# Attention's P·V as f32 products on four column strips, with the turned probabilities leaving PSUM once

## What is computed

```python
# layer 1 (layer 3 is the same with a causal mask instead of bias and src_mask)
scores = jnp.einsum('bhqd,bhkd->bhqk', q / math.sqrt(HEAD_DIM), k)
scores = scores + attention_bias
scores = jnp.where(src_mask, -jnp.inf, scores.astype(jnp.float32))
probs = jax.nn.softmax(scores, axis=-1).astype(v.dtype)
ctx = jnp.einsum('bhqk,bhkd->bhqd', probs, v)
x = x + (ctx @ Wo + bo)
h = _ln(x) * g2 + beta2
ff = _gelu2(h @ W1 + b1) @ W2 + b2
```

## Time and profile before

| | us |
|---|---|
| three runs, median | 2738.48 |
| lowest and highest | 2730.14, 2739.05 |
| the profiled execution: span | 2737.0 |
| PE busy | 2599.0 (95%) |
| PE weight loads busy | 2214.0 (81%) |
| ACT busy | 2338.8 (85%) |
| DVE busy | 2221.9 (81%) |
| POOL busy | 1674.0 (61%) |

### The profile page before, as it was taken

One profiled execution on the slowest core, in us unless ns is written; L12 is line 12 of the kernel. 1 busy time (PEld: TensorE's weight loads), 2 busy tenths in 40 slices (PEclk: granted clock), 3 DMA queues, 4 the chain that ended last, 5 costly groups with the idle time before them and its releaser, 6 DMA issues.

```text
span 2737.0 us, 62626 instructions
## 1 busy us (share of the span) xinstructions
PE 2599.0 (95%) x20072; PEld 2214.0 (81%) x20072; DVE 2221.9 (81%) x7925; ACT 2338.8 (85%) x5285; POOL 1674.0 (61%) x1742
## 2 busy tenths in 40 slices
PE   8888999999999999999999999999999999999987
PEld 7766888888888888888888888888888888888776
DVE  5668888888888888888888888888888888888753
ACT  1567899999999999998999989999998998999865
POOL 2666666766667675666666566666666666765431
PEclk8988999999999999999999999999999999999999
DMA  6433343333333333333333333343333333333211
GB/s 230 130 96 102 91 118 108 116 102 113 96 103 115 109 114 103 110 98 101 114 112 112 103 108 101 98 119 108 113 97 114 101 100 116 109 105 102 63 31 29
DMA packets 176549, 287.96 MB, mean 105 GB/s; under 512 B 45856, under 2 KB 99104, under 8 KB 175840
## 3 DMA queue, kind: packets, MB, share of 16 engines
q1 hardware_dynamic: 176224, 283.97, 35.2%
HBM read 174.64 MB, written 8.45 MB: 67 GB/s over the span
## 4 chain that ended last, share of the span: by engine, by line
PE 71%; ACT 13%; issue 4%; SPq 4%; DVE 3%; POOL 2%; DMA 2%; ACTq 0%; DVEq 0%; POOLq 0%
PE bank L1171 15%; PE bank L1178 14%; PE bank L1199 10%; PE bank L1156 9%; PE bank L1148 8%; PE bank L1191 5%; ACT PB L990 3%; PE bank L1163 3%; SPq L411 2%; ACT PH L996 2%; PE bank L1306 2%; ACT BB L1011 2%; PE bank L1217 2%; PE bank L1218 2%; ACT AA L1011 2%
## 5 line engine op out<-in xcount | busy, mean ns | idle before, releaser
L990 ACT ACTIVATE PB<-PB,mx 128x256 f32<-128x256 f32 (+1 forms) x2048 | 834.6, 475 | 6.0 <-DVE mx L786 5.2
L794 DVE TENSOR_TENSOR PO<-bank,PH 128x384 f16<-128x384 f32 (+1 forms) x1024 | 589.4, 616 | 247.5 <-ACT PH L996 244.4
L497 POOL TENSOR_TENSOR BT<-BT,MN 128x1024 f32<-128x1024 f32 x256 | 545.9, 2137 | 174.2 <-DMA BT<-in_bias 173.4
L996 ACT ACTIVATE PH<-bank 128x384 f16<-128x384 f32 (+1 forms) x1024 | 499.0, 538 | 127.7 <-PE bank L1199 127.2
L1191 PE MATMUL bank<-Ks,Qs 96*128 96x512 f32 (+1 forms) x1024 | 519.1, 510 | 19.5 <-DMA Ks<-KU 11.9
L1199 PE MATMUL bank<-ident,PB 128*128 128x128 f32 x3584 | 484.8, 275 | 8.5 <-ACT PB L990 4.5
L1199 PEld LDWEIGHTS bank<-ident,PB 128*128 128x128 f32 x3584 | 421.2, 142 | 46.8 <-ACT PB L990 12.3
L786 DVE CUSTOM_DVE_ANT_0 PB<-bank,BT 128x256 f32<-128x256 f32 x1024 | 386.7, 416 | 37.6 <-PE bank L1191 36.2
L786 DVE CUSTOM_DVE_ANT_0 PB<-bank,caus 128x128 f32<-128x128 f32 (+1 forms) x1024 | 321.0, 351 | 22.9 <-PE bank L1191 22.5
L1217 PEld LDWEIGHTS bank<-VP,PH 128*128 128x128 f16 x3584 | 204.0, 96 | 119.2 <-issue 93.5
L1171 PE MATMUL bank<-TN,Wf 128*128 128x256 f32 x1024 | 253.9, 391 | 16.6 <-ACT BB L1011 11.4
(11 more groups left out here) (225 smaller groups left out, 5208.8 us busy)
## 6 DMA issues: line engine op xcount, KB each, us to landing
BT<-in_bias SPq DMA_DIRECT2D x256, 512.0 KB, 3.9
Qs<-QH SPq DMA_DIRECT2D x512, 64.0 KB, 2.4
Ks<-KH SPq DMA_DIRECT2D x1024, 32.0 KB, 2.0
Qs<-QU SPq DMA_DIRECT2D x256, 64.0 KB, 2.5
Ks<-KU SPq DMA_DIRECT2D x512, 32.0 KB, 2.0
XT<-in_xT SPq DMA_DIRECT2D x32, 256.0 KB, 2.9
X<-in_x SPq DMA_DIRECT2D x32, 256.0 KB, 2.9
AB<-ada_rows SPq DMA_DIRECT2D x32, 256.0 KB, 3.6
```

Source lines behind the costliest of these rows:

```text
L497: G.op.tensor_tensor(v2(BT[k % 4]), v2(BT[k % 4]), MN[:, :].unsqueeze(1).broadcast_to([128, 2, 512]), ALU.add).then_inc(g_bt, 1)
L794: V.op.tensor_tensor(PO[i][:, 0:w], bP[h][:, 0:w], PH[i][:, 0:w], ALU.subtract).then_inc(v_low, 1)
L990: S.op.activation(o, o, ACT.Exp, scale=-1.0, bias=mx[u.layer][:, c:c + 1]).then_inc(a_exp, 1)
L996: S.op.activation(PH[i][:, 0:w], bP[h][:, 0:w], ACT.Copy).then_inc(a_high, 1)
```

## The change

What it does:

- **One copy out of PSUM.** `high` and `low` are gone. The turned probabilities of head 0 are copied by ACT (`ev0`), those of head 1 by DVE (`ev1`), each once, in f32, into a ring of six tiles `PT` (`flipped`).
- **P·V turned round.** Once for a pair, `pv` issues for each half k of the keys four f32 products: the stationary side is a head's 128x32 slice of `VW` (16 channels of V and 16 columns of ones), the moving side its turned probabilities, 256 queries wide (128 in the second half of layer 3, where the causal mask leaves nothing else). The four (two units x two heads) go to four column strips of the array, `tile_position=(0, 32*s)`, and to 32 partitions each of one half of the bank `bV`.
- **A turn back.** The result has channels on partitions, so ACT copies it out (`cx`, into `ET`) and PE turns it (`ct`, two f32 transposes of 128x128 per pair) before `pvn`, which is now a reciprocal and one product.
- **V is not split.** `v_hi`, `v_sub`, `v_mid`, `v_lo` are gone; `v_out` writes f32 into `VW`.
- **Room.** `PT` needs SBUF, so `FY` becomes `XT`, `MB` becomes `TN`, `MC` becomes `AA[3]` and `TC` becomes `BB[3]` (`AA[3]` in the last batch), with five new waits: `ld_x` also waits for `v_n2`, `t2_out` for `p_w3`, `t4_out` for `p_w1`, `c3_out` for `p_w4`, and `v_out` for `p_pv` of the batch before.
- **Ticks.** All numbers of `P` and `OWN` are new, and a small table `SPLIT` gives layer 3 its own ticks for five pieces.

```diff
-    "score0": -2, "score1": 0, "bias0": 1, "bias1": 3, "exp0": 3, "exp1": 6, "flip0": 7, "flip1": 7,
-    "high0": 8, "high1": 8, "low0": 10, "low1": 10, "pv0": 12, "pv1": 12, "pvn": 15,
+    "score0": -2, "score1": 1, "bias0": -1, "bias1": 2, "exp0": 2, "exp1": 5, "flip0": 7, "flip1": 7, "ev0": 8,
+    "ev1": 8, "pv": 12, "cx": 13, "ct": 15, "pvn": 16, "ld_bt": -10, "mask_add": -10, "stack": -8, "ld_x": -97,
...
-                for h in range(2):
-                    for u in unit_at(t, f"low{h}"):
-                        i, w = (2 * u.D + h) % 4, 128 * len(blocks(u.layer))
-                        V.wait_ge(a_high, head_of(u.D, h))
-                        V.wait_ge(p_pv, head_of(u.D - 2, h))
-                        V.op.tensor_tensor(PO[i][:, 0:w], bP[h][:, 0:w], PH[i][:, 0:w], ALU.subtract).then_inc(v_low, 1)
+                for u in unit_at(t, "ev1"):
+                    w = 128 * len(blocks(u.layer))
+                    V.wait_ge(p_flip, head_of(u.D, 1))
+                    V.wait_ge(p_pv, flipped_free(u.D))
+                    V.op.tensor_copy(flipped(u.D, 1)[:, 0:w], bP[1][:, 0:w]).then_inc(v_ev, 1)
...
-                        V.op.tensor_reduce(rd[:, :].rearrange("p (g d) -> p g d", d=16),
-                                           pv[:, :, 0:48].rearrange("p g (k d) -> p g d k", k=3), AX.X,
-                                           ALU.add).then_inc(v_pvn, 1)
...
-                        S.op.activation(PH[i][:, 0:w], bP[h][:, 0:w], ACT.Copy).then_inc(a_high, 1)
+                for u in unit_at(t, "ev0"):
+                    w = 128 * len(blocks(u.layer))
+                    S.wait_ge(p_flip, head_of(u.D, 0))
+                    S.wait_ge(p_pv, flipped_free(u.D))
+                    S.op.activation(flipped(u.D, 0)[:, 0:w], bP[0][:, 0:w], ACT.Copy).then_inc(a_ev, 1)
+                for u in unit_at(t, "cx"):
+                    if u.n % 2 == 1:
+                        J = u.D // 2
+                        S.wait_ge(p_pv, J + 1)
+                        S.wait_ge(p_ct, J - 1)
+                        S.op.activation(ET[J % 2][:, :], half(bV, J % 2), ACT.Copy).then_inc(a_cx, 1)
...
-                                T.op.matmul(bV[:, o:o + 49], PH[i][:, c * 128:c * 128 + 128], vv, start=(n == 0), stop=False)
-                                last = T.op.matmul(bV[:, o:o + 49], PO[i][:, c * 128:c * 128 + 128], vv, start=False,
-                                                   stop=(n == len(ks) - 1))
+                        T.wait_ge(a_ev, u.D + 1)
+                        T.wait_ge(v_ev, u.D + 1)
+                        T.wait_ge(v_pvn, 2 * (J - 1) + 2)
+                        for k in range(2):
+                            q = 128 if k == 1 and x == 3 else 0
+                            for s in range(4):
+                                et, h = s // 2, s % 2
+                                v = (k * 16 + 8 * et + 2 * j + h) * 32
+                                last = T.op.matmul(half(bV, J % 2)[32 * s:32 * s + 32, q:256], VW[x][:, v:v + 32],
+                                                   flipped(u.D - 1 + et, h)[:, k * 256:k * 256 + 256 - q],
+                                                   start=(k == 0), stop=(k == 1), tile_position=(0, 32 * s))
+                        last.then_inc(p_pv, 1)
+                for u in unit_at(t, "ct"):
+                    if u.n % 2 == 1:
+                        J = u.D // 2
+                        T.wait_ge(a_cx, J + 1)
+                        for q in range(2):
+                            last = T.op.transpose(half(bV, J % 2)[:, q * 128:q * 128 + 128], ET[J % 2][:, q * 128:q * 128 + 128],
+                                                  ident[:, :])
+                        last.then_inc(p_ct, 1)
```

158 lines of the change are left out of this document (65 added, 93 removed), and 111 rows, old and new, of tables (OWN, P).

## The result

The changed kernel takes 2752.50 us (median of 3 runs, 2752.05 to 2753.03) against 2738.48. The ratio is 1.0062, with a 95% interval of 1.0043 to 1.0082: 14 us slower. I had forecast 57 us slower. The sign is right and the size is not: the new work of PE costs some 40 us more than I took, and PE's gaps close by some 84 us more than I took.

What follows compares the result with a forecast made beforehand. PE was taken as the bound, by what it must stream. The terms 10 + 56 + 10 - 19 + 22 - 12 - 10 gave +57 us, about 2795 against 2738; the 8-in-10 range was 2670 to 3040.

Steps and rivals of the forecast that it cites:

- P·V itself: PE's P·V products: 183 us removed, 193 added if the four strips stream side by side, +10 us.
- Weight loads: Sixteen 32-column loads per pair on PE, estimated at 0.03 us each, under the streaming time: no cost.
- Entering and leaving the strips: 512 changes of PE's array shape, at twice the score's 0.02 us, less 10 us paid before: +10 us.
- The turn back: 512 added transposes of 0.109 us on PE, with nothing to hide them: +56 us.
- o3: PE's wait for ACT's copy of the turned CX goes, with the drain before it: 0.6 us per batch, -19 us.
- t4: PE's wait at t4 grows by 0.7 us per batch, half of the chain's queueing assumed gone: +22 us.
- The feed-forward waits: PE's waits between feed-forward groups, 15.4 us in 25 batches, halve with a freer ACT: -12 us with the hidden part.
- The three gap terms: Changes in PE's gaps at o3, at t4 and between feed-forward groups: -19, +22 and -12 us.
- the gaps close: Rival: over 2.4 of PE's 7 us of gaps per batch go, making the kernel faster, 2670 to 2702 us; chance 0.31.
- The ends: At the run's start and end, where PE is busy 39 of 50 us, less ACT and DVE work gives -10 us.
- Half parallel: Rival: strip records start in program order, P·V takes 427 us, total 3010; chance 0.20, shared with being bound by loads.
- not parallel: Rival: the strips stream one after another, P·V takes 771 us instead of 193, total about 3370; chance 0.08.

Runs made afterwards that it cites:

- the exchanged loops: The changed kernel with P·V's loops swapped, strip outside and half of the keys inside: 2756.5 us, ratio 1.0071.
- the exchanges: New arithmetic in old order 3204.0 us, old arithmetic in new order 3676.4; only the places behind attention swapped: changed kernel 3006.0, kernel before 3396.9.

## Why the prediction was right or wrong

- **P·V itself (+10).** The decision for parallel strips was right, and blocks of 0.65 to 0.86 us were nearly so: 0.69 and 0.91 us without the exit, +22. What is missing is 0.02 us between the first and the last strip's start and a first step of 0.240 instead of 0.215.
- **Weight loads (0).** The result holds, the reason does not. I had estimated 0.03 us for a load of 32 columns from its size. It takes 0.109 (the group below), where the records of wide loads have 0.142 (flips) and 0.190 (products): a quarter of the columns is more than half of the time. That lies at my "as much as a long one", by which P·V would have been bound by its loads at 450 us. It is not, because four loads run side by side, as the products do: 4096 x 0.109 = 446 us of loads in 107 us of busy time.

```profile
L1220 PEld LDWEIGHTS bank<-PT,VW 128*32 128x32 f32 x4096 | 107.3, 109 | 109.8 <-issue 61.7
```

- **Entering and leaving the strips (+10): mis-sized.** I took 0.04 us, twice the score's 0.02, from a row that changes rows and not columns. It is 0.093 at each end, 512 x 0.093 = +48, less the 10 that were paid before by my reckoning. The bounds of 0 to 0.17 held it. The rule of the Trainium skill (TensorEngine Tiling (Array Packing), Key Properties) that a change of mode drains the array spoke for a price, and there is one; by it I had +77. The term measures +38, between the two, with 0.093 us at each end where a full drain would be 0.17.
- **The turn back (+56): wrong in its last step.** The 512 x 0.109 are there. That nothing hides them is wrong: leaving them out gives 11 us.
- **`o3` (-19): right.** Its wait is gone, with a P·V block as cover.
- **`t4` (+22): too high.** I had expected a wait of about 1.5 us. It rose from 0.82 to 1.04 us per batch, since the chain from `o3` lost nearly all its queueing on DVE and POOL, not half. What I did not see is the second end of this wait, ACT's own queue behind PE's flips.
- **The feed-forward waits (-12): too small.** They have not halved, they are gone in the waits of the stretch. By the table they and their hidden part went from 1.7 to 0.5 us per batch, some -37 us over the run.
- **The step that failed.** The three gap terms together were -9 us, 0.3 us per batch. Measured are 3.0 us per batch. I counted the gaps that the waits list names, 47 us in 25 batches, and left the other 5 us per batch of the earlier trace rows's sum as they were, without a reason. By the table 1.2 us went ahead of the feed-forward groups, 0.7 ahead of P·V, 0.6 at `o3`, 0.3 at a projection and 0.5 in small ones, and 0.2 came at `t4`. P·V and the projection had no term in my sum. With more work for ACT than before, only the feed-forward part comes back. The rival "the gaps close" named this mechanism and its point of decision, more than 2.4 us per batch, and 3.0 went. It did not win because the bill was higher than in my sum: P·V +22, changes of shape +38, turn back +56 are 116 us, 3.6 per batch, not 76. With the 76 of my sum and the gaps as they are, it would take 40 us less, 2712. Two errors stood against each other: 40 us too little work, and some 84 too few gaps closed (3.0 x 31 - 9). That the sign came out right is luck in part: with my bill of work and the gaps as they closed it would have been the other one. My own sign of being wrong, gaps under 5 us per batch, came up with 3.8.
- **The ends (-10): about half of it.** 9.6 us are gained at the start. At the end the tail is 12.3 shorter, but the last two periods are 15.4 and 1.3 longer, since pieces of the tail now stand in the first of them: 4 us lost. Together -5.
- **The rivals of order.** "Half parallel" and "not parallel" fall, with the row of the four starts and with the exchanged loops.

Where the gaps closed is measured; through which part of the change each of them closed stays open, since the order can't be taken apart, as the exchanges show. That the feed-forward gaps need spare time of ACT is shown for this order, how much of it is not; what the old order could make of the full spare time of both engines is not shown either.

## What to carry to other kernels

Where each engine's order is a fixed list, the price of work on the busiest engine depends on its place: 56 us of transposes in front of waits cost 11, while of some 88 us of changes of shape and small products ahead of P·V (0.35 a pair) 65 showed. Such a table and the arithmetic are one thing: old with new lost 250 to 940 us, and single moves of a tick lost 14 to 25, so that a change of the arithmetic has to be judged with an order made for it. And before a chain is shortened, look at the waiting engine's own queue: the last releaser may stand behind work that the waiter itself has yet to send. Last, when an engine is loaded for a test, look at the spread of the added instructions and at the whole run's busy time, not at their mean and the share of a stretch: here the one hid holds of 2.3 us, the other 100 us too much.

## What the runs showed of the hardware

- Products on four column strips start 7 ns apart and stream fully side by side, each strip in its own order: a record of another strip passes records ahead of it in the program. With the four of a strip next to each other the starts are 13 ns apart and the block is 0.02 us longer.
- A change between the full array and the strips costs PE 0.093 us, in either direction, behind records that stream 0.109 or 0.215 us. From the start of a full record of two columns to the first start on a strip it was 0.18 us, and 0.10 from a strip record of two columns to the full array.
- A load of 32 columns takes 0.109 us, and four of them run at once; the records of wide f32 loads have 0.142 and 0.190.
- The `tensor_tensor` of 224 f32 columns with both operands (the same tile) and the result in SBUF took 0.38 us on DVE. Where it started while POOL was in an instruction of more than 1 us, it ended at the earliest 0.25 us after that instruction: 213 of the 214 that took over 0.5 us in one kernel ended just then, after up to 2.31 us. The ACT copy of the same 224 columns took 0.37 to 0.41 us, whatever POOL did.
